# GpSimd copies both following heads' values first and stores the output tile last

## The reference

```python
def wl_step(acc, wl):
    cpm, iw = wl
    m = cpm[None, :, None, None]
    Qw = Q * m
    Kw = K * m
    scores = jnp.einsum('bhqd,bhkd->bhqk', Qw, Kw) * SCALE
    scores = scores * jnp.cos(KERR * scores * scores)
    attn = jax.nn.softmax(scores, axis=-1)
    out = jnp.einsum('bhqk,bhkd->bhqd', attn, V)
    return (acc + out * iw, None)
...
x = _layernorm(x + attention(x))
# h = gelu(x @ w1[e]), y = h @ w2[e], out = sum of gates[e] * y[e] + gates[8] * x
x = _layernorm(x + experts(x))
```

## Time and profile before

| | us |
|---|---|
| median of 3 runs (7534.82 to 7537.15) | 7535.9 |
| the profiled execution, whole | 7540.05 |
| its span, first to last instruction | 7538.4 |
| ScalarE busy | 7184.6 (95%) |
| TensorE busy, matmuls | 5560.1 (74%) |
| VectorE busy | 5456.0 (72%) |
| GpSimd busy | 44.4 (1%) |

### The profile page before, as it was taken

One profiled execution on the slowest core, in us unless ns is written; L12 is line 12 of the kernel. 1 busy time (PEld: TensorE's weight loads), 2 busy tenths in 40 slices (PEclk: granted clock), 3 DMA queues, 4 the chain that ended last, 5 costly groups with the idle time before them and its releaser, 6 DMA issues.

```text
span 7538.4 us, 124074 instructions
## 1 busy us (share of the span) xinstructions
PE 5560.1 (74%) x43972; PEld 2013.9 (27%) x43972; DVE 5456.0 (72%) x9488; ACT 7184.6 (95%) x2227; POOL 44.4 (1%) x112
## 2 busy tenths in 40 slices
PE   6767767677777777777777777777777777777777
PEld 2222222222222222222222222222222222222225
DVE  4767677767777777777777777777777777777763
ACT  4999999999999999999999999999999999999992
POOL 0000000000000000000000000000000000000000
PEclk7999999999999999999999999999999999999998
DMA  2000000000000000000000000000000000000000
GB/s 57 4 4 4 2 4 4 3 3 9 28 25 28 17 26 23 19 28 19 29 28 16 25 28 16 26 28 16 28 30 17 26 27 14 28 17 26 27 12 34
DMA packets 40422, 151.80 MB, mean 20 GB/s; under 512 B 7969, under 2 KB 26273, under 8 KB 33441
## 3 DMA queue, kind: packets, MB, share of 16 engines
q1 hardware_dynamic: 39072, 142.13, 5.7%
q0 software_dynamic: 768, 1.57, 0.1%
HBM read 132.66 MB, written 11.01 MB: 19 GB/s over the span
## 4 chain that ended last, share of the span: by engine, by line
ACT 44%; issue 29%; PE 12%; DVE 8%; ACTq 6%; DMA 1%; DVEq 0%; POOLq 0%; SPq 0%; POOL 0%
ACT ring L522 43%; PE pv L593 8%; ACTq L517 4%; DVE scores L724 2%; DMA out<-tile_out 1%; DVE vprobs L747 1%; ACTq L518 1%; DVE tile_z L810 1%; PE sc L1042 1%; PE tr L1050 1%; PE sc L648 1%; DVE qt L718 0%; DVE tile_small L360 0%; DVE tile_small L359 0%; DVE tile_small L361 0%
## 5 line engine op out<-in xcount | busy, mean ns | idle before, releaser
L522 ACT ACTIVATE ring<-scores 128x4096 f32<-128x4096 f32 (+3 forms) x2048 | 6979.3, 3497 | 144.5 <-PE pv L593 109.3
L593 PE MATMUL pv<-ring,vh 128*32 128x512 f32 x31744 | 4010.8, 635 | 1702.1 <-ACT ring L522 1574.4
L593 PEld LDWEIGHTS pv<-ring,vh 128*32 128x32 f32 x31744 | 1003.7, 115 | 4350.8 <-ACT ring L522 2189.0
L754 DVE COPY numer<-pv 128x512 f32<-128x512 f32 x512 | 353.6, 691 | 1067.7 <-PE pv L593 1062.4
L747 DVE SCALAR_TENSOR_TENSOR vprobs<-vprobs,vrest 128x512 f32<-128x512 f32 x1536 | 1063.8, 693 | 52.3
L714 DVE TENSOR_REDUCE rowmax<-sc 128x1 f32<-128x1024 f32 x512 | 602.5, 1219 | 120.8 <-PE sc L556 120.8
L724 DVE COPY scores<-sc 128x1024 f32<-128x1024 f32 (+1 forms) x512 | 601.6, 1217 | 59.0 <-PE sc L575 58.4
L593 PE MATMUL pv<-vprobs,vh 128*32 128x512 f32 x1024 | 530.3, 599 | 0.0
L745 DVE TENSOR_TENSOR vprobs<-vprobs,vrest 128x512 f32<-128x512 f32 x512 | 354.7, 693 | 17.6
L741 DVE SCALAR_TENSOR_TENSOR vrest<-vpower,vrest 128x512 f32<-128x512 f32 x512 | 354.6, 693 | 17.6
L748 DVE SCALAR_TENSOR_TENSOR vprobs<-vprobs,vpower 128x512 f32<-128x512 f32 x512 | 354.5, 692 | 17.4
(11 more groups left out here) (156 smaller groups left out, 2408.2 us busy)
## 6 DMA issues: line engine op xcount, KB each, us to landing
tile_w<-in_L_ffn_w SPq DMA_DIRECT2D x48, 2048.0 KB, 7.6
qt<-q_scratch SPq DMA_DIRECT2D x256, 36.0 KB
kt_<-k_scratch SPq DMA_DIRECT2D x256, 36.0 KB
ring<-in_L_ffn_w SPq DMA_DIRECT2D x2, 2048.0 KB, 11.5
scores<-in_L_attn_x SPq DMA_DIRECT2D x4, 512.0 KB, 4.9
q_scratch<-qt SPq DMA_DIRECT2D x4, 512.0 KB, 3.9
k_scratch<-kt_ SPq DMA_DIRECT2D x4, 512.0 KB, 4.2
v_scratch<-vv SPq DMA_DIRECT2D x4, 512.0 KB, 3.5
```

The costliest lines, as they stand in the source:

```text
L522: nc.scalar.activation(ring[:, i % SLOTS, 0:cols], scores[:, bass.ds(n % 2, 1), half * CK:(half + 1) * CK, :].rearrange("p o k s -> p (o k ...
L593: last = nc.tensor.matmul(pv[g * VC:(g + 1) * VC, pair % 2, :], vh[:, buf, half * CK + k, :], probs, start=(half == 0 and k == 0), stop=(h ...
L754: nc.vector.tensor_copy(numer[:, pair, :], pv[:, pair, :]).then_inc(pv_read, 1)
```

## The change

In each pair with a tile GpSimd made: copy for head n into buffer 0, copy for head n + 1 into buffer 1, store of the tile. It now makes: copy for head n + 1 into buffer 1, copy for head n + 2 (the next pair's first) into buffer 0, store of the tile. The copy for head 16 stands ahead of the loop, and the last pair, which has no next one, is written out behind it. The waits in `copy_values` and those around the store are the same.

```diff
@@ pool_main
             with pool.Fori(1, FIRST_PAIR) as i:
                 copy_values(pool, 2 * i, 0)
                 copy_values(pool, 2 * i + 1, 1)
-            with pool.Fori(0, PAIRS - FIRST_PAIR) as i:
-                copy_values(pool, 2 * (i + FIRST_PAIR), 0)
+            copy_values(pool, H, 0)
+
+            def store_tile(i, last=False):
                 copy_values(pool, 2 * (i + FIRST_PAIR) + 1, 1)
+                if not last:
+                    copy_values(pool, 2 * (i + FIRST_PAIR) + 2, 0)
                 pool.wait_ge(tile_done, i + 1)
                 pool.dma_start(out_tiles[bass.ds(i, 1)].rearrange("o p e -> p (o e)"), tile_out[:, :]).then_inc(tile_stored, 16)
                 pool.wait_ge(tile_stored, 16 * (i + 1))
                 pool.sem_inc(tile_out_free, 1)
+            with pool.Fori(0, PAIRS - FIRST_PAIR - 1) as i:
+                store_tile(i)
+            store_tile(PAIRS - FIRST_PAIR - 1, True)
```

## The result

The changed kernel takes 7582.5 us (median of 4 runs, 7579.3 to 7593.3), the kernel before 7536.5 (7534.8 to 7539.2): a ratio of 1.0063, 95% interval 1.0048 to 1.0078. It is 46 us slower, where 52 us less were forecast. The profiled execution took 7584.06, its span is 7582.5, 44.1 over the span before.

The account below looks back on a forecast made before the run. ScalarE was taken to bound the kernel, waiting at 23 pair boundaries for GpSimd's late value copies. Of 86.4 us there, 2.3 would stay and 32.4 be given back: 51.7 gained, 7484.2 us median, 8-in-10 range 7447 to 7516.

Parts of the forecast that it names:

- The copy for the next pair is off the path: GpSimd's copy moved ahead of the store, some 109 us before the boundary, was costed at nothing.
- What is late next at the boundary: Between pairs, TensorE's first value matmuls would start right after its last transposes, ending 2.78 us ahead of ScalarE at full clock.
- The residue: ScalarE's wait left at each boundary between pairs: 0 to 0.15 us, 2.2 at worst; taken as 0.1, 2.3 us over 23.
- The second wait: ScalarE's wait at chunk 20 of a pair's first head; forecast to average 2.12 us over 23 pairs, giving back 32.4 us.
- the middle: Mean of the two sizes seen at chunk 20 of a pair's first head, 0.57 and 3.67 us: 2.12 us.
- The sum: Boundary waits of 86.4 us less 2.3 left there and 32.4 given back at chunk 20: 51.7 us gained.
- (b): Rival: ScalarE's wait at chunk 20 of the first head becomes 3.67 us in every pair; gain 16.1, 7519.8 us; chance 0.19.
- the end ones: The first and last pair with a tile, whose waits at chunk 20 of the first head were 3.62 and 3.71 us.
- (c): Rival: low clock meets the tile's products at the boundary (2.2 us) and chunk 20 (3.7); slower, 7569 us; chance 0.03.
- Its point of turning: The kernel turns slower once ScalarE's waits at the boundary and at chunk 20 together pass 4.47 us per pair.

Follow-up runs that it names:

- e2: The kernel before, with TensorE's tile loop cut one head later so that it turns between the two heads of a pair: 7535.7 us, ratio 0.9998.
- e1: The changed kernel, with TensorE's tile loop cut one head later so that it turns between the two heads of a pair: 7503.4 us, ratio 0.9953.
- e3: The changed kernel plus a GpSimd copy of a constant behind the landed store, for which TensorE waits at each pair's start: 7542.8 us, ratio 1.0007.

## Why the prediction was wrong, step by step

*The copy for the next pair is off the path, the store isn't held up, SyncE isn't either.* Right: no wait for `vh`, copies 106 to 110 us early, store 0.7 us behind `tile_out` as before.

*What is late next at the boundary: "TensorE can begin when its last transposes are done".* This is the step that failed. The residue was put at 0 to 0.15 us, 2.2 at most, and is 77.0 / 22 = 3.5, because the return of TensorE's loop takes 3.0 to 3.7 us in the same place. I took the copy for the whole of the 4.31 us idle, since the profile puts a wait down to what came last; that something else ends only 0 to 1 us earlier can't be seen in that row. Nor were the two independent: without the return the copy would have come after 2.9 us (e2), not 4.3. It could be seen in the trace of before at the boundaries without a tile (the row at 347.45 above), which I looked at only for ScalarE's small waits. The schedule by hand was right in itself: at the last boundary, where nothing turns, the group begins at 7182.62, right behind the transposes, takes the 3.64 reckoned with, and ScalarE doesn't wait.

*The second wait grows once the pairs are no longer held at the same place against the clock.* Right in kind, and also that it would be the waits taken away that had held it. The 23 pairs behind the first gave 65.0 - 3.6 = 61.4 us against the 48.8 of the sum, or 2.67 a pair for 2.12. It took no values between; it is one of two, 0.57 or 3.6 to 3.9, and 15 of the 23 took the high one. Taking the middle was a guess between two ends. The clock behind it (stretches of TensorE, changed kernel: three of the long pair, one of the short one before it), and the two slow groups of the long pair behind its first:

```profile
core 0: us, PE busy (x), PEclk, DMA share, GB/s
4645.50:4652.20 6.70, 5.85 (x28) 0.50 0.01 4
4672.80:4679.50 6.70, 5.71 (x28) 0.50 0.01 2
4703.50:4710.30 6.80, 5.39 (x26) 0.51 0.00 0
4474.80:4478.20 3.40, 3.40 (x24) 0.51 0.00 0
```

```profile
4673.79 6.46 PE L599 MATMUL pv<-ring,vh 128*32 128x512 f32 x32 [2.30 <-ACT ring L528]
...
4705.44 5.99 PE L599 MATMUL pv<-ring,vh 128*32 128x512 f32 x32
```

In the long pair the clock is at 1.2 GHz and not 2.4 in a stretch in the middle too; the group there takes 6.46 at 4673.79, the VectorE chain starts that much later, and the group at its end takes 5.99 (5.34 in the short pair). It is the picture of the first and last pair of before, in two of three pairs.

*The sum.* 86.4 - 2.3 - 32.4 = 51.7 gained was forecast. Measured: the boundary gave 86.4 - 77.0 = 9.4, the second place took 65.0 - 20.0 = 45.0.

*The rivals.* (b), that all pairs become like the end ones, is what happened in two pairs of three, but it had the boundary's gain beside it. (c), the side on which it ended, was priced for the wrong mechanism: `tile_part_two` never ran at the low clock at the boundary (its 16 matmuls took 1.95 to 2.05 us in all pairs). Its point of turning was right: a long pair waits 3.4 + 3.9 = 7.3, a short one 3.65 + 0.57 = 4.2, and the mean of them lies over 4.47. I gave it 0.03, since my cases let the boundary's gain stand wherever the copy came early. A rival that left this gain out because two causes overlay each other was missing.

The Trainium skill (Runtime: NRT & Kernel Launch, section Instruction fetch mechanics) says that a taken branch breaks the sequential prefetch of instructions: where its target isn't among the instructions already at hand, execution stalls until it is fetched. The gaps of 3.0 to 3.7 us at every return in the changed kernel, and none where the loop is left, agree with it; that it is the fetch and not another part of the return wasn't tried.

## What to carry to other kernels

Before a wait is costed as gained, look at the same place where its cause is absent: the same loop boundary in another phase, the first and the last turn. A second, shorter wait behind the first shows itself only there. A loop's return belongs where the neighbour engine has slack, or between stages and not at the tightest one; here moving it was worth 79 us in the changed kernel (7582.5 to 7503.4), with the same work in the same order, and nothing in the kernel before (7535.7), where GpSimd's copy still held the boundary. And where several engines run in step, an edit that only shifts a start can cost more than it saves, if a chain elsewhere has no slack for the slow clock: first give the chain slack, then take the waits away.

## What the runs showed of the hardware

- TensorE idled 3.0 to 3.7 us at each return of its `Fori` loops in the changed kernel, with bodies of two heads with a tile and without one, and 3.3 to 4.5 at the place of e1. It idled for nothing of the kind when it ran out of the tile loop into the code behind it (7182.62).
- A store of 64 KB by GpSimd took 2.9 to 3.8 us to land when TensorE's loop turned at the same time, and 1.8 to 1.9 (2.2 once) when it didn't. ScalarE's loops around the quads turn without such a gap (rows of 16 merged chunks of 54.5 us with no idle time between).
- In the 72 pairs of three traces (before, changed, e3) a low-clock stretch of TensorE that began 26 to 40 us after the pair's first group went with all 22 second waits over 3.5 us and with none of the 50 others. Idle time ahead of that group of 3.57 us or more went with 0.54 to 0.60, of 2.80 to 3.40 with 3.6 to 3.9, so 0.2 us of a start went with over 3 us later on; in e2 the same second wait of 0.57 came with 2.9.
- A wait without use made the changed kernel 0.5% faster (7582.5 to 7542.8).
